# Node chain's scalar steps moved from VectorE to GpSimd, and a new order for the last stage

## The reference

```python
h = relu(layernorm(x)); x = x + L0(h, adj, adj)   # layer 0: filter network on each edge
h = relu(layernorm(x)); x = x + L1(h, adj)        # layer 1: hyperbolic attention
h = relu(layernorm(x)); x = x + L2(h, adj)        # layer 2: D^-1/2 A D^-1/2 x W + b
h = relu(layernorm(x)); x = x + L3(h, adj)        # layer 3: mean of messages, update
```

```python
res = tanh(mxn / xn * artanh(xn)) * mx / mxn      # mobius_matvec, c = 1
h = proj(res); h = proj(mobius_add(h, hyp_bias))  # norms, one tanh, one logarithm, four divisions
```

## Time and profile before

| what | us |
|---|---|
| median of three runs | 2719.68 |
| profiled execution, span (its own time) | 2700.1 |
| first silu of the last stage starts | 1553.3 |
| `a_att` of slot 7 (after the last silu) starts | 2591.9 |
| DVE busy in the span | 2208.6 |
| POOL busy in the span | 1765.0 |
| ACT busy in the span | 2064.3 |

### The profile page before, as it was taken

The page is one execution under the profiler, slowest core; times in us unless marked ns, Lnnn a source line. Parts: engine busy times, 40 slices in busy tenths (PEclk is TensorE's granted clock), DMA queues, the critical chain, the costliest instruction groups (busy, mean ns, idle before and its releaser), DMA issues. The chain is left out here.

```text
span 2700.1 us, 63006 instructions
## 1 busy us (share of the span) xinstructions
PE 2388.6 (88%) x25296; PEld 1171.0 (43%) x25296; DVE 2208.6 (82%) x3763; ACT 2064.3 (76%) x1938; POOL 1765.0 (65%) x1149
## 2 busy tenths in 40 slices
PE   4899999999999999999996388889898989888863
PEld 2333333333333333333333254545555555545543
DVE  6699898998989989899897865769898989875556
ACT  6888888888888888888884277778777777767741
POOL 0799888998989989889893244445454545455421
PEclk8999999999999999999998699989999989999986
DMA  8899999998989999899971356756575757575530
GB/s 234 176 201 202 195 199 193 199 201 194 203 193 200 198 195 203 194 200 200 196 166 31 92 118 103 135 94 145 91 148 93 154 92 142 94 134 95 95 59 20
DMA packets 312066, 410.26 MB, mean 152 GB/s; under 512 B 91488, under 2 KB 284640, under 8 KB 286688
## 3 DMA queue, kind: packets, MB, share of 16 engines
q1 hardware_dynamic: 311776, 406.23, 72.6%
HBM read 368.38 MB, written 35.65 MB: 150 GB/s over the span
## 5 line engine op out<-in xcount | busy, mean ns | idle before, releaser
L684 POOL TENSOR_TENSOR f_gate<-rfT,f_sq 128x1024 f32<-128x1024 f32 x512 | 1217.6, 2378 | 225.0 <-DVE f_prod L699 151.7
L617 PE MATMUL PS<-f_h,w_W2T 64*64 64x512 f32 x8192 | 998.1, 591 | 10.0 <-PE PS L617 1.8
L699 DVE SCALAR_TENSOR_TENSOR f_prod<-PS,b2l,f_gate 128x1024 f32<-128x1024 f32 x512 | 657.4, 1284 | 145.1 <-PE PS L617 109.3
L1195 ACT ACTIVATE a_silu<-PS,c_att_b 128x1024 f32<-128x1024 f32 x512 | 545.3, 1110 | 221.0 <-PE PS L1023 218.2
L579 ACT ACTIVATE f_h<-PS,c_b 128x1024 f32<-128x1024 f32 x512 | 556.2, 1113 | 165.8 <-PE PS L599 165.0
L691 DVE TENSOR_REDUCE yT<-f_prod 128x16 f32<-128x1024 f32 x512 | 618.8, 1209 | 0.0
L617 PEld LDWEIGHTS PS<-f_h,w_W2T 64*64 64x64 f32 x8192 | 341.2, 133 | 560.4 <-issue 435.9
L1337 POOL TENSOR_TENSOR a_outer<-a_by_i,a_by_j 128x256 f32<-128x256 f32 x512 | 356.3, 722 | 326.0 <-PE PS L1023 312.8
L599 PE MATMUL PS<-f_gauss,W1two 64*64 64x512 f32 x4096 | 545.8, 594 | 6.7 <-ACT f_gauss L566 4.8
L1023 PE MATMUL PS<-a_outer,a_rows 32*128 32x128 f32 x8192 | 389.7, 297 | 116.7 <-ACT a_silu L1195 82.0
L1023 PEld LDWEIGHTS PS<-a_outer,a_rows 32*128 32x128 f32 x8192 | 316.6, 196 | 328.6 <-issue 138.3
(11 more groups left out here) (242 smaller groups left out, 2123.0 us busy)
## 6 DMA issues: line engine op xcount, KB each, us to landing
f_gauss<-in_adj SPq DMA_DIRECT2D x128, 1024.0 KB, 11.7
f_sq<-adj_sq SPq DMA_DIRECT2D x256, 512.0 KB, 8.8
a_rows<-hw_d SPq DMA_DIRECT2D x1024, 64.0 KB
hw_d<-b_xc SPq DMA_DIRECT2D x16, 512.0 KB, 4.5
hw_d<-b_sq SPq DMA_DIRECT2D x16, 512.0 KB, 6.4
b_x<-in_x SPq DMA_DIRECT2D x8, 512.0 KB, 4.3
x_d<-b_x SPq DMA_DIRECT2D x8, 512.0 KB, 5.9
h_d<-b_h SPq DMA_DIRECT2D x8, 512.0 KB, 4.1
```

Source lines behind the costliest of these rows:

```text
L617: PE.matmul(post("message", c)[rows[b], n, :], W2T[rows[k], rows[fh]], hidden(c, n)[rows[k], b, :], start=not second, stop=bool(second)).t ...
L684: GP.tensor_tensor(by_pair(GATE[c % GATE_BUFS][:]), rf, by_pair(squares), ALU.mult).then_inc(s_gate, 1)
L699: V.scalar_tensor_tensor(PR[c % PR_BUFS][:], post("message", c).rearrange("p b n -> p (b n)"), b2l[:, c % 2:c % 2 + 1], GATE[c % GATE_BUFS ...
L1195: A.activation(SI[p % SI_BUFS][:], PS[:, first:first + 2, :].rearrange("p b n -> p (b n)"), ACT.Silu, bias=cols["att_b1"][:]).then_inc(s_s ...
```

## The change

1. In `lead`, nearly all scalar steps go from DVE to POOL (`own_l = Order(o_lp)` in the POOL program). DVE keeps the sums, the copy of `d` (now with a factor 2), and the reciprocals: one over four rows (`izm`, `izr`, `i1`, `i2`) and one of `s17`. Two semaphores (`divs`, `divided`) lead to and from the first, two (`s17`, `s17_inv`) to and from the second, and `sum3` starts POOL.
2. Operations that DVE does in one instruction with a scalar and two operands are two instructions on POOL.
3. All due numbers of the last stage are new, monotone within each chain, and stand in one table (`STEPS`); `FILLS` and `SHIFT` are new too. Ticks have 64 parts and not 16.
4. Chains are made one slot earlier, so that a step may be due ahead of its slot; on SP, some steps that stood behind one number have numbers of their own (the load of `fam` and `ftm`, now 37 ticks before its slot and behind a wait for `av`; the load of `fH`; the two halves of `att`; `u`).

```diff
-SHIFT = {("lead", 0): -4.25, ("lead", 1): 8.875, ("lead", 2): 4.5, ("pair", 0): -3.1875, ...
-FIRST_SLOT, PARTS = -2, 16
+SHIFT = {
+    ("last", 0): -0.0625, ("last", 1): -0.125, ("last", 5): -0.25, ("last", 6): -0.875, ("last", 7): 4.75,
+    ("lead", 0): -25.9375, ("lead", 1): -0.1875, ("lead", 2): 0.125, ("lead", 7): 0.0625, ...
+FIRST_SLOT, PARTS = -2, 64
...
+    ("act", "last"): (3.875, 15.3125, 15.6875, 24.5, 29.4375, 29.625, 35.375, 35.6875, 37.4375, 41.25),
+    ("act", "mix"): (13.5625, 13.6875, 23.375, 23.8125, 24.1875, 25.125, 25.625, 26, 27.625, 37.875, 49.75,
+        55.5, 57.5, 61.0625),
+    ("act", "pair"): (15.125, 15.125, 15.125, 17.5625, 17.875, 18.8125, 19.4375, 19.5, 21.5, 25.3125, 26.625),
+    ("act", "lead"): (31.6875, 33.375, 39.375, 39.375, 41, 41.0625, 49.6875, 57.1875),
+    ("pool", "lead"): (47.375, 47.4375, 49.5625, 49.8125, 50, 50.125, 50.125, 50.5, 53.9375, 53.9375,
+        57.0625, 59.4375, 61.6875, 63.1875, 63.1875, 65.0625, 66.1875, 66.1875, 66.6875, 69.3125,
+        71.8125, 71.8125, 73.25, 75.8125),
+    ("dve", "lead"): (1.4375, 1.75, 15.1875, 30.0625, 32.5625, 43.0625, 43.0625, 44.1875, 45, 46.3125,
+        62, 72.125, 73.125),
...
# POOL, new (all of it runs as single instructions, each behind a wait for the one before)
+        def ts(o, i, s1, op0, s2=None, op1=None, gives=()):
+            own_l.before(GP)
...
+        def rsqrt_step(o, minus_half, sq):
+            tt(sq, o, o, MU)
+            tt(sq, sq, minus_half, MU)
+            ts(sq, sq, 1.5, AD)
+            tt(o, o, sq, MU)
+
         def lead(g):
...
+            GP.wait_ge(b["sum3"], g + 1)
+            ts(sB("var"), sB("var"), 1.0 / P, MU, LN_EPS, AD)
+            ts(sB("r2", 2), sB("r2", 2), MIN_SQ, MA)
+            rsqrt_start(sB("rstd", 3), sB("var", 3), sB("h1", 3))
+            for _ in range(3):
+                yield next(at)
+                rsqrt_step(sB("rstd", 3), sB("h1", 3), sB("w1", 3))
...
+            ts(sB("zr"), sB("z"), 0.1, MA, 2.0, MU, gives=(b["divs"], g))
...
+            GP.wait_ge(b["divided"], g + 1)
+            tt(sB("ratio"), sB("o"), sB("izm"), MU, gives=(b["ratio"], g))
...
# DVE: what is left of the scalar steps
+            V.tensor_scalar(sB("d4"), line(num["d"])[:, 0:GT], 2.0, None, MU).then_inc(*takes(num["d"]))
+            yield next(at)
+            V.wait_ge(b["divs"], g + 1)
+            recip(sB("izm", 4), sB("zm", 4), gives=(b["divided"], g))
+            yield next(at)
+            V.wait_ge(b["s17"], g + 1)
+            recip(sB("s17"), sB("s17"), gives=(b["s17_inv"], g))
-            yield -110.3125
-            rsqrt(sB("s19"), sB("s18"), sB("h1"), sB("w1"))
...
```

More of the change, by code:

```diff
@@ L721 @@
 FILLS = {
[9 rows of a table removed]
+    "lead": (
+        ("y0", -13.0625), ("y1", 2.5), ("t0", 30.3125), ("t1", 36.25), ("m0", 39.125), ("m1", 40.0625), ("d",
+        42.375),
+    ),
+    "pair": (
+        ("h0", 15.125), ("h1", 15.25), ("g", 17.125), ("y", 17.25), ("r0", 18.9375), ("r1", 18.9375), ("r2",
+        18.9375), ("r3", 20.5),
+    ),
+    "mix": (
+        ("u0", 7.125), ("u1", 10.1875), ("v0", 23.4375), ("v1", 23.8125), ("s0", 24.375), ("s1", 24.8125),
+        ("a0", 25.3125), ("a1", 25.8125), ("z0", 26.0625), ("z1", 26.125),
+    ),
@@ L761, in run @@
     live = []
-    for slot in range(FIRST_SLOT, GROUPS + 3):
-        live += [Paced(chains[c](slot + ahead), slot * TICKS + SHIFT.get((c, slot + ahead), 0)) for c, ahead in AHEAD.items() if 0 <= slot + ahead < GROUPS]
+    for slot in range(FIRST_SLOT - 1, GROUPS + 3):
+        live += [Paced(chains[c](slot + 1 + ahead), (slot + 1) * TICKS + SHIFT.get((c, slot + 1 + ahead), 0))
+                 for c, ahead in AHEAD.items() if 0 <= slot + 1 + ahead < GROUPS]
         for tick in range(TICKS):
@@ L769, in run, with steps @@
         live = [chain for chain in live if chain.due is not None]
+def steps(engine, chain):
+    return iter(STEPS[engine, chain])
 def fill_numbers():
@@ L936, in pair @@
         def pair(g):
+            at = steps("sp", "pair")
             nodes = slice(g * GT, (g + 1) * GT)
-            yield 12.9375
+            yield next(at)
             taken(SP, number["pair", g, "r3"])
@@ L964, in mix @@
         def mix(g):
+            at = steps("sp", "mix")
             nodes = slice(g * GT, (g + 1) * GT)
-            yield -244.8125
+            yield next(at)
+            before(SP, f["av"], g)
             SP.dma_start(fam[:], d["adj"][:, nodes, :]).then_inc(d_adj, 16)
             SP.dma_start(ftm[:], d["adjT"][:, nodes, :]).then_inc(d_adj, 16)
+            yield next(at)
             SP.wait_ge(d_h, (g + 1) * 16)
@@ L991, in last @@
         def last(g):
+            at = steps("sp", "last")
             nodes = slice(g * GT, (g + 1) * GT)
-            yield 13.875
+            yield next(at)
             if g + 1 < GROUPS:
@@ L1209, in lead @@
         def lead(g):
+            at = steps("act", "lead")
             num = numbers("lead", g)
-            yield 25.25
+            yield next(at)
             A.wait_ge(b["xc"], g + 1)
@@ L1232, in pair @@
         def pair(g):
+            at = steps("act", "pair")
             num = numbers("pair", g)
             for h in range(2):
-                yield (5.0625, -26.125)[h]
+                yield next(at)
                 evacuate(num[f"h{h}"], half(bHT, h))
-            yield -1.4375
+            yield next(at)
             for h in range(2):
@@ L1295, in last @@
         def last(g):
+            at = steps("act", "last")
             num = numbers("last", g)
-            yield 2.375
+            yield next(at)
             if g:
@@ L1349, in pair @@
         def pair(g):
+            at = steps("pool", "pair")
             num = numbers("pair", g)
-            yield 14.5625
+            yield next(at)
             taken(GP, num["y"])
@@ L1390, in last @@
         def last(g):
+            at = steps("pool", "last")
             X = fXs[g % 2]
-            yield -12.375
+            yield next(at)
             if g:
@@ L1460, in lead @@
         def lead(g):
+            at = steps("dve", "lead")
             num = numbers("lead", g)
@@ L1490, in lead @@
-            yield -93.9375
+            rsum(sB("m2"), bH[:], gives=(b["sum3"], g))
+            yield next(at)
             filled(V, num["d"])
[L1492 to L1499, removed]
@@ L1572, in pair @@
         def pair(g):
+            at = steps("dve", "pair")
             num = numbers("pair", g)
@@ L1602, in pair @@
             for quarter in range(4):
-                yield (-39.5625, -141.1875, -13.125, 14.4375)[quarter]
+                yield next(at)
                 n = num[f"r{quarter}"]
@@ L1774, in last @@
         def last(g):
+            at = steps("dve", "last")
             num, s, X = numbers("last", g), sG(g), fXs[g % 2]
             ts, tt, stt, recip, rsum, series, blend, rsqrt = ops(own_e)
-            yield -179.4375
+            yield next(at)
             V.wait_ge(f["csq"], 2 * g + 1)
@@ L1813, in last @@
                 V.tensor_tensor(X[:, two, :], bank(n, 2 * P)[:, :, P:2 * P], X[:, two, :], AD).then_inc(*takes(n))
-            for name, scale, first in (("q", "has", 36), ("e", "ideg", 39)):
+            for name, scale in (("q", "has"), ("e", "ideg")):
                 for h in range(2):
-                    yield {36: (43.0625, 47.125), 39: (-85.0625, 52.8125)}[first][h]
+                    yield next(at)
                     n = num[f"{name}{h}"]
```

462 lines of the change are left out of this document (279 added, 183 removed), and 9 rows, old and new, of the table FILLS.

## The result

The changed kernel takes 2719.4 us (median of 20 runs) and the kernel before, beside it, 2715.1: a ratio of 1.0022 (95% interval 1.0012 to 1.0032), some 6 us of 2715. That is no change by the bound set above, and 21 us from the 2698 that I forecast. The profiled execution has a span of 2717.2 us where before had 2700.1. In every execution that has both on record the time is some 2 us above the span (2719.4 for this one), and not equal to it as I wrote ahead of the prediction. So the changed kernel was profiled at its median and the kernel before some 13 us under its own, and most of these 17 us (11 by the ratio, 13 by the medians) are the difference between two single executions.

What follows compares the result with a forecast made beforehand. It took silus waiting for PE, and chain steps that don't fit those gaps, as the slots' bound, not DVE. Terms -39 - 5 + 7 - 2 + 17 made -22 us: 2719.7 becomes 2698, forecast 2670 to 2706, range 2655 to 2745.

Steps and rivals of the forecast that it cites:

- the bound set above: Whole kernel: a measurement can tell about 0.5%, or 14 us, from no change.
- The slots' gaps: Slots 0 to 7: chain steps spread wider over the sets and shared table loads save 39 us, about 5.5 each full slot.
- The `a_rows` wait: PE's 17.7 us wait for loads queued on SP behind the `hw` stores shrinks: -5 us (0 to -17).
- lead(0): Start, before the first silu: 84 POOL steps of 0.26 us plus 1.0, less VectorE's 15.6, cost +7 us.
- lead(1): Start: 45 POOL steps ahead of the first outer product, first silu at 1551.7: -2 us (-5 to +10).
- ACT at the logarithm: Slots 0 to 5: ACT and every silu wait 2.9 us a slot for POOL's chain: +17 us (0 to +45).
- one of the signs that I had named: Full slots: the prediction is wrong if they stay at 133 us, where near 127 was expected.
- The third: Rival, slots: the gap count fails, new waits take back the gain, slots keep 133 us: 2725 us, chance 0.13.
- the gap count: Slots: each set charged the largest of 3.19 us, ACT's and PE's work; full slots 126.1 us against 131.6 before.
- The fourth: Rival, slots: DVE was the bound after all, 15 us less in six slots, some -85: 2635 us, chance 0.05.
- The first: Rival: POOL late at the logarithm, small steps 0.5 us and more or behind DVE instructions: +40, 2760 us, chance 0.20.

Runs made afterwards that it cites:

- sp_three: The changed kernel with SP's `by_i` loads behind the `a_rows` load at tick 41, `fat` loads behind that at 9, VectorE's `fat` product due 14.5: 2680.6 us, ratio 0.9889.
- ln_apart: The changed kernel with ACT's logarithm of mix due at 50.5 and not 49.75, one silu behind the leading chain's: 2738.4 us, ratio 1.0094.
- three_dve: The changed kernel with all eight leading chains' scalar steps on VectorE, in the new order, and SP's `by_i` and `fat` loads moved behind `a_rows` loads: 2700.5 us, ratio 0.9961.
- sp_fat: The changed kernel with SP's store of `att`, 16 loads of `fat` and load of `fH` back at tick 1.94, not 6.375: 2714.8 us, ratio 1.0020.
- old_order_pool: The kernel before, in its own order, with only the leading chain's scalar steps moved to POOL and VectorE taking `c1` at tick 54.5: 2843.2 us, ratio 1.0484.

## Why the prediction was wrong, by its steps

- *The slots' gaps, -39 us.* Right, once no load is late: first silu to last `a_att` takes 1038.6 us before, 1007.2 in sp_three, 1002.1 and 1000.6 with the start on VectorE, that is -31, -36 and -38. These are single executions, and that of before lies 13 us under its median, so the gain may be larger. ln_apart shows some 20 of it to be the shared table loads. But I credited the order alone, at no value for VectorE's relief. three_dve shows that the order needs the move: without it the slots come to 1044.
- *The `a_rows` wait, -5 (0 to -17).* This is the step that failed. It looked at one thing in front of the loads, the stores of `hw`, which do stand behind a load now and do little harm (SP waits 73.5 us there, but tile 3 and 4's loads are in time). It asked neither when PE would come to each tile in the new order nor what else stands in SP's list. For tile 2 the list is no worse: `fat`'s due number rose from 1.94 to 6.375, but its 16 issues stood ahead of the load before too, and sp_fat shows that 1.94 changes nothing. What changed is PE, which the emptied gaps bring there 4 to 8 us earlier, before its data. So the gaps' gain and this wait are not two separate terms, as my sum had them. For tile 6 the load is later: `by_i` stands at 37.06 for a `VT` due on POOL at 39.62, where before it was due at 39.375 and SP had no wait for `VT`. The runs put 25 and 17 us on the two, 38.9 together in the slots: +36 to +42 in place of -5, and with it the whole gain. The slots stayed at 133, one of the signs that I had named. 34.8 of the 38.9 us are PE's wait (52.0, and 17.2 in sp_three). The rest may go with the clock: the sum named under the logarithms is 42 us in the changed kernel and 33 in sp_three.
- *lead(0), +7.* The mechanism was right, the size low: +10.1 (25.9 against 15.9 us from the end of the last sum to the multiplication with `c1`). POOL's trace has 84 steps where VectorE had 75. The line through POOL's products gave 0.20 for a step of 8 columns, and a product takes that; but many `tensor_scalar` steps take 0.23 to 0.26, steps of 24 columns 0.22 to 0.29, and a dependent successor starts 0.09 later and not 0.06. 0.306 us a step is 1.5 times VectorE's 0.205. The rule of the Trainium skill ("GPSIMD Engine Reference", "Engine selection") that GpSimd is some two times slower with two inputs would have given an estimate of 0.40. No row here bears it out for tiles this small, where by the line through rows 9 some 0.18 of a step's 0.20 us don't grow with the columns.
- *lead(1), -2.* Small, as I had it, but -0.3: the filter ends 2.4 us later, of which 1.4 are left at lead(0)'s last sum; with lead(0)'s 10.1 that leaves -0.3 of the first silu's 11.1. POOL did start 1.8 us behind `U`, but its 45 steps took 14.0 us, 0.31 each, and not 11.7.
- *ACT at the logarithm, +17.* Did not appear. ACT has no wait of 1 us for `ratio` in a full slot. I gave POOL 7.6 us from its tick 47.4 to ACT's 49.7. In the slot of 1958 it had 15.2 (2047.12 to 2062.34): some 5 of them are PE's stall, and POOL's ticks run two sets ahead of ACT's. I used that lead for the outer products and not for the chain.
- *Rivals.* The third (slots keep 133 us, as new waits take what the gaps give back; 2725, at 0.13) is what happened, the waits being `a_rows`; its reason, that the gap count does not hold, is not. The fourth is half right, by three_dve. The first did not happen here, but its mechanism, outer products stuck behind POOL's waiting chain, is what old_order_pool shows.
- The sum with what was measured, in the profiled executions: -31 for the slots without late loads, +39 for these, +11.1 up to the first silu, -1.5 behind the last `a_att`: 17, as their spans say. 2.4 of it is the filter's end, and where the 13 us lie by which the profiled execution of before is under its median, no run shows.

## What to carry to other kernels

When an order of steps is worked out anew, ask first where it makes the bound engine quicker, and whether its loads are there that much earlier. Then go through the in-order DMA queue step by step: for each load that the bound engine waits for, add up the issue time and the waits of all that stands between its predecessor and it. As an estimate from this queue, loads that take 6.4 us in every 16.5 leave room for one burst of 8, and only right behind a load. A burst whose data come late is moved behind the next load; here an earlier due number did nothing (sp_fat). A chain is moved to a slower engine where something hides it, and left on the faster one where nothing does: that alone was 15 us here.

## What I had not expected of the hardware

Two stalls of 3 to 4 us on PE were followed by 3.4 and 6.1 us of granted clock at 1.2 GHz, in which 32 products took 2.09 us and not 1.35, while behind nine others of the 18 they took 1.17; the three full slots that ran at 1.00 took 126.5 to 128.6 us. And 16 issues of `a_rows` take SP 6.4 us, yet where PE waited at tiles 2 and 6, with `fat` or `by_i` loads issued just before, its products followed the last issue by another 3.3 to 6.8. So such a load needs 10 to 13 of its 16.5 us, by an estimate from these rows.
